# A fused pre-norm decoder layer: experts' units over the whole period, third layer norm and gate in halves, residual in two buffers

## The chip, the cores and the metric

One core of a Trainium2 chip runs the kernel. The metric is the device time of one execution in microseconds, the median of several runs. TensorE multiplies matrices into PSUM, VectorE, ScalarE and GpSimd compute elementwise (the first two read PSUM), and SyncE starts the loads. Each engine works through its own queue in order and waits for the others on semaphores.

## What is computed

The reference takes x of 128 sequences x 64 tokens x 128 features and a context of the same shape. Cut to what matters:

```
x = x + agent_attention(layernorm(x))            # 16 heads of 64, 8 agents per sequence, two softmaxes
x = x + cross_attention(layernorm(x), context)   # 16 heads of 8, causal mask, softmax
x = x + experts(layernorm(x))

def experts(x):
    scores = softmax(x @ gate_w.T)               # 16 experts in 4 groups of 4
    # a group counts the sum of its two best; the two best groups stay;
    # in them the two best experts get their softmax score as weight
    h = silu(x @ We1 + be1) * (x @ We3 + be3)    # 64 wide, each of the 16 experts
    y = sum over experts of weight * (h @ We2 + be2)
    z = (silu(x @ ws1 + bs1) * (x @ ws3 + bs3)) @ ws2 + bs2   # shared expert, 128 wide
    return y + z
```

All experts are computed for all tokens; the weights of those not chosen are zero.

## The kernel before

A group is 16 sequences, 1024 tokens, eight tiles of 128 tokens, and there are eight groups. `run` (L287) calls each engine's `both(e, g)` for nine periods: (None, 0), then (e, e + 1) for e = 0 to 6, then (7, None). In a period the experts of group e run beside the attentions of group g; `nxt` is the group after g, whose first steps (context, first layer norm, agent's moments M) are prepared at the end. The order of each engine's queue is the order of the calls in its `both`, written by hand: TensorE's at L714, ScalarE's at L959, VectorE's at L1256, GpSimd's at L398.

The experts' work is 18 units, nine for each half of the tokens: unit k = 0 and 9 are the shared expert, the others a pair of experts. `unit` (L518) calls `up` (six matmuls of 512 columns, two PSUM banks H1 and H3, high and low parts of the operands apart), `weight` (one matmul that spreads the pair's weights, bank C) and `down_to` of the unit before (eight matmuls; the ninth unit adds the bias; bank Y). `silu` (L882) is ScalarE's part, `hidden` (L1152) VectorE's: `hidden_3` adds the bias and multiplies, `weighted` multiplies by the weights.

Before the units come the third layer norm and the gate, for all eight tiles at once: `norm("e")`, GpSimd's power, `apply("e")`, the turn into xnT3, the scores, `gate_shift` (L1090), ScalarE's exponential, `gate` (L1098: groups, two rounds of the best expert, weights), the turn of the weights (L755). The attention's steps are, in order: values V, `scores_1`, `scores_2` with `soften`, the keys KT with `K_moved`, the turn of the probabilities with `normalise_2`, `pool_tokens`, the agent's values UT, U, `Ya`, the second layer norm `norm("a")` with `apply("a")`, the turn xnT2, the queries QT, four `scores(u)` with `maxima` (row maxima from four banks), the shifts' turn mT, four rounds of `scores_T`, exponentials, `values`, `turn_O`, `project`.

PSUM has eight banks. `RINGS` gives each tile a bank of a ring and `wait_free` makes TensorE wait until the tile before it in that bank was read. Attention has a ring of four; H1, H3, C and Y have one bank each. Outside the units the four are lent: H1 and H3 to the next group's context, xn and M (ring f), C to mT, O, OT (ring o), Y to Yx. So no unit can run while the transposed scores run: units 13 to 16 stand between the four `scores(u)`, and 17 behind them. The residual is xr, the residual after cross-attention xe, and the result is written into xn3's buffer (xo).

## Time and profile before

| what | value |
|---|---|
| median of 3 runs | 1292.38 us (1291.53 to 1292.47) |
| profiled execution | 1290.0 us, span 1288.3 us |
| TensorE matmul busy | 1069.6 us, 83% |
| VectorE busy | 646.9 us, 50% |
| ScalarE busy | 456.3 us, 35% |
| GpSimd busy | 116.5 us, 9% |
| mean granted clock of TensorE | 0.878 of 2.4 GHz |
| loads of ScalarE's tables | 16 of 1.28 us |

The span goes from the first to the last instruction. The busy times are shares over stages with different limits, so the stages are read one by one: windows give each engine's busy time in a stretch, the list of waits says what released an engine, the timeline shows single instructions with the idle time before them. A granted clock of 1.0 is 2.4 GHz, of 0.5 1.2 GHz; a mean between them is a mixture of the two.

### The profile page before, as it was taken

The page shows a single profiled execution, that of the slowest core. Times are in us where ns is not written, and L with a number is a line of the kernel's source. Part 1 is how long each engine was busy: PE and PEld are TensorE (multiplying, and loading weights), DVE is VectorE, ACT ScalarE, POOL GpSimd, SP SyncE. Part 2 cuts the span into 40 slices and gives each one's busy share as a digit, 9 for nine tenths or more (in the row PEclk, how much of TensorE's full clock was granted, in tenths as well). Part 3 has the DMA queues.
Part 4 walks back from the last instruction along what each step waited for, and adds up shares of the span by engine and source line. Part 5 has one row for each costly group of instructions (what it writes and reads, how often), then busy time and mean ns, then how long its engine had stood idle before and what let it go on. Part 6 is the DMA issues. An engine that isn't in the chain of part 4 may idle for free.

```text
span 1288.3 us, 26430 instructions
## 1 busy us (share of the span) xinstructions
PE 1069.6 (83%) x11562; PEld 892.9 (69%) x11629; DVE 646.9 (50%) x1633; ACT 456.3 (35%) x790; POOL 116.5 (9%) x117
## 2 busy tenths in 40 slices
PE   6657879988798969988799887989699887998687
PEld 5644767787676858677676876768586776767565
DVE  2535276624657166542757246571665427561353
ACT  4432453234422353234432344223432345322221
POOL 7100010002000020001000020000200010000100
PEclk9788889978899889988899788998899888995589
DMA  6100010001000010000100010000100000000000
GB/s 164 34 1 2 2 34 1 10 10 34 1 9 10 2 34 1 10 10 2 34 9 2 10 34 1 9 10 2 33 1 10 10 2 1 9 10 2 1 1 17
DMA packets 28404, 18.50 MB, mean 14 GB/s; under 512 B 7393, under 2 KB 26882, under 8 KB 28290
## 3 DMA queue, kind: packets, MB, share of 16 engines
q1 hardware_dynamic: 26402, 12.35, 3.6%
q0 software_dynamic: 1280, 4.20, 1.1%
q8 instruction: 92, 1.51, 0.5%
q10 hardware_dynamic: 608, 0.27, 0.1%
q14 instruction: 22, 0.18, 0.0%
HBM read 12.62 MB, written 4.19 MB: 13 GB/s over the span
## 4 chain that ended last, share of the span: by engine, by line
PE 65%; DVE 20%; ACT 7%; POOL 4%; issue 3%; DVEq 0%; another core or an unknown queue 0%; POOLq 0%; ACTq 0%
PE banks L508 8%; PE banks L651 6%; PE banks L634 5%; PE banks L497 4%; PE banks L498 4%; PE banks L499 4%; PE banks L695 3%; DVE xn L1086 3%; PE banks L539 3%; PE banks L467 3%; ACT PXUT L943 3%; PE banks L626 3%; DVE sil L1172 2%; PE banks L604 2%; PE banks L775 2%
## 5 line engine op out<-in xcount | busy, mean ns | idle before, releaser
L887 ACT ACTIVATE sil<-banks,b 128x512 f32<-128x512 f32 x144 | 99.5, 691 | 247.2 <-PE banks L499 244.5
L508 PE MATMUL banks<-w,hT 128*128 128x128 f32 x1152 | 156.7, 280 | 29.1 <-DVE xn L1185 18.0
L1172 DVE SCALAR_TENSOR_TENSOR sil<-banks,b,sil 128x512 f32<-128x512 f32 x128 | 95.8, 748 | 167.1 <-ACT sil L887 154.9
L508 PEld LDWEIGHTS banks<-w,hT 128*128 128x128 f32 x1152 | 153.5, 196 | 31.6 <-DVE xn L1185 18.5
L1240 DVE RECIPROCAL rx<-banks 128x32 f32<-128x32 f32 x32 | 11.4, 358 | 243.1 <-PE banks L651 243.1
L943 ACT ACTIVATE PXUT<-banks 128x512 f32<-128x512 f32 x128 | 69.4, 609 | 154.8 <-PE banks L634 154.8
L1179 DVE TENSOR_TENSOR hT<-sil,banks 128x512 f32<-128x512 f32 x128 | 88.0, 687 | 15.1 <-remote 11.0
L1223 DVE TENSOR_REDUCE mx<-banks 128x8 f32<-128x512 f32 x128 | 79.5, 684 | 26.5 <-PE banks L604 26.5
L467 PE MATMUL banks<-ident,xn 128*128 128x128 f32 x192 | 38.2, 365 | 56.5 <-DVE xn L1086 56.5
L497 PE MATMUL banks<-xnT3l,w1h 128*128 128x512 f32 x144 | 77.7, 540 | 7.6 <-ACT sil L887 6.4
L695 PE MATMUL banks<-pooled,A 128*128 128x128 f32 x512 | 73.6, 303 | 12.2 <-ACT M L880 10.3
L396 POOL TENSOR_TENSOR norm_a<-norm_a,mhalf 128x8 f32<-128x8 f32 x16 | 26.5, 1656 | 623.2 <-DVE norm_a L1078 623.2
L651 PE MATMUL banks<-Vx,PXUT 128*64 128x18 f32 x2048 | 79.1, 228 | 2.9 <-ACT PXUT L943 2.9
L651 PEld LDWEIGHTS banks<-Vx,PXUT 128*64 128x64 f32 x2048 | 75.9, 162 | 7.6 <-issue 5.1
L634 PEld LDWEIGHTS banks<-KQ 32*128 32x128 f32 x2048 | 74.7, 226 | 8.5 <-issue 8.5
L695 PEld LDWEIGHTS banks<-pooled,A 128*128 128x128 f32 x512 | 69.4, 216 | 15.3 <-ACT M L880 12.9
L634 PE MATMUL banks<-KQ 32*128 32x64 f32 x2048 | 79.5, 314 | 0.0
L467 PEld LDWEIGHTS banks<-ident,xn 128*128 128x128 f32 x192 | 31.5, 191 | 59.2 <-DVE xn L1086 36.3
L497 PE MATMUL banks<-xnT3l,w3h 128*128 128x512 f32 x144 | 61.5, 427 | 5.2 <-DVE sil L1172 4.5
L498 PE MATMUL banks<-xnT3h,w1l 128*128 128x512 f32 x144 | 60.6, 421 | 0.0
L499 PE MATMUL banks<-xnT3h,w1h 128*128 128x512 f32 x144 | 60.0, 417 | 0.0
L498 PE MATMUL banks<-xnT3h,w3l 128*128 128x512 f32 x144 | 58.0, 403 | 0.0
(203 smaller groups left out, 1858.3 us busy)
## 6 DMA issues: line engine op xcount, KB each, us to landing
xin<-in_x SPq DMA_DIRECT2D x8, 512.0 KB, 4.5
cin<-in_ctx SPq DMA_DIRECT2D x8, 512.0 KB, 5.8
out_x<-xn POOLq DMA_DIRECT2D x16, 256.0 KB, 2.8
KQ<-in_L_attn_Wqkv SPq DMA_DIRECT2D x3, 512.0 KB, 5.2
KQ<-in_L_ffn_We SPq DMA_DIRECT2D x2, 512.0 KB, 4.3
KQ<-in_L_attn_Wo SPq DMA_DIRECT2D x1, 512.0 KB, 7.9
w<-in_L_ffn_We SPq DMA_DIRECT2D x1, 512.0 KB
KQ<-in_L_ffn_ws SPq DMA_DIRECT2D x2, 64.0 KB, 4.4
```

The costliest lines, as they stand in the source:

```text
L467: last = turn_over(ps(name)[:, P * t:P * t + P], src[:, 4 * n + t, :], ident[:])
L497: mm(ps(name)[:], wh[:, 2 * p:2 * p + 2, :], xl, start=True, stop=False)
L498: mm(ps(name)[:], wl[:, 2 * p:2 * p + 2, :], xh, start=False, stop=False)
L499: mm(ps(name)[:], wh[:, 2 * p:2 * p + 2, :], xh, start=False, stop=True).then_inc(fulled(name), 1)
L508: mm(ps(name)[:, P * t:P * t + P], hT[:, k % 2, P * t:P * t + P], w2[:, pair[k], :], start=(n == 0 and t == 0), stop=False, skip_group_che ...
L634: last = mm(ps(name)[:, c0:c0 + S], Kx[rr, j, b, :], Qx[rr, S * b:S * b + S], start=False, stop=True, skip_group_check=True, tile_position ...
L651: last = mm(ps(name)[64 * r:64 * r + 64, o0:o0 + w], PT[:, XQ * (u % 2) + j // 2, c0:c0 + S], Vx[:, 4 * u + k, j, :], start=True, stop=True)
L695: last = mm(ps(f"M_{n}")[:, P * k:P * k + P], A[:, 4 * (n % 4) + k, :], pooled[:], start=True, stop=True)
L887: nc.scalar.activation(sil[:, k % 2, :], ps(f"H1_{k}")[:], ACT.Silu, bias=b1[:, pair[k]:pair[k] + 1]).then_inc(sil_ready, 1)
L943: nc.scalar.activation(PT[:, k % (2 * XQ), :], ps(f"ST_{k}")[:], ACT.Exp).then_inc(ex_ready, 1)
L1172: V.scalar_tensor_tensor(sil[:, k % 2, :], ps(f"H3_{k}")[:], b3[:, p:p + 1], sil[:, k % 2, :], ALU.add, ALU.mult).then_inc(hid_ready, 1)
L1179: V.tensor_tensor(hT[:, k % 2, :], sil[:, k % 2, :], ps(f"C_{k}")[:], ALU.mult).then_inc(hT_ready, 1)
```

## The change

1. The four banks of attention serve all of attention, the third layer norm's turn, the gate and the weights' turn; H1, H3, C and Y belong to the units alone. `attention_tiles` writes out the order of the tiles for every period.
2. The units are spread: `unit(e, 0)` opens the period, units 14 to 17 stand in the four rounds of transposed scores.
3. Third layer norm and gate work on halves of four tiles. Half 0 of group g is done at the end of the period in which g's cross-attention ends; half 1 at the start of the next one. `gate` is split into `gate_groups`, `gate_best` (twice) and `gate_weights`.
4. The residual has two buffers by turns, xr[g % 2], in which the sums are made in place; xe and xo are gone.
5. The keys (`keys_of`, `K_moved`) move behind unit 9, the next group's first norm and its turn move ahead of the transposed scores.

```diff
+        if e is None:
+            add(g, "ctxT_0", "ctxT_1", "xnT1_0", "xnT1_1", *[f"M_{k}" for k in range(8)])
+        add(g, *[f"V_{k}" for k in range(4)])
+        add(e, "xnT3_1")
+        add(g, "s1_0", "s1_1", "s2_0")
+        add(e, "combS_0", "gate_1")
...
+        for u in range(UX):
+            add(g, *[f"ST_{XQ * u + q}" for q in range(XQ)])
+            if u:
+                add(g, f"OT_{u - 1}")
+            add(g, f"O_{u}")
+            if u == UX - 1:
+                add(g, "xnT3_0")
+            add(n, f"M_{2 * u}", f"M_{2 * u + 1}")
+            if u:
+                add(g, f"Yx_{u - 1}")
+        add(g, "gate_0", f"OT_{UX - 1}", f"Yx_{UX - 1}")
```

TensorE's order, from the start of a period:

```diff
+                unit(e, 0)
                 if g is not None:
                     pe.wait_ge(ctxT_ready, 2 * g + 2)
                     for n in range(4):
                         values_of(g, n)
                 if e is not None:
+                    turn_3(e, 1)
...
+                    turn_weights(e, 0)
+                unit(e, 1)
+                if e is not None:
+                    gate_scores(e, 1)
                 if g is not None:
                     scores_1(g, 2)
                     scores_1(g, 3)
                     scores_2(g, 1)
+                unit(e, 2)
+                unit(e, 3)
+                if g is not None:
+                    turn_probs(g, 0)
+                unit(e, 4)
...
+                unit(e, 9)
                 if g is not None:
                     keys_of(g, 0)
                     keys_of(g, 1)
+                unit(e, 10)
                 if g is not None:
                     pe.wait_ge(xn_ready, 2 * g + 2)
                     four(g, "xnT2_0", xn, 0)
                     four(g, "xnT2_1", xn, 1)
                 unit(e, 11)
...
+                    queries(g)
+                unit(e, 12)
+                if g is not None:
                     pe.wait_ge(Kx_ready, 2 * g + 2)
+                    scores(g, 0)
+                    scores(g, 1)
+                unit(e, 13)
+                if g is not None:
+                    scores(g, 2)
+                    scores(g, 3)
+                    if nxt is not None:
+                        front_ctx(nxt)
+                        front_xn(nxt)
+                    turn_shifts(g)
+                    pe.wait_ge(V_ready, 4 * g + 4)
                 for u in range(UX):
                     if g is not None:
+                        scores_T(g, u)
+                    unit(e, 14 + u)
+                    if g is not None:
+                        if u:
+                            turn_O(g, u - 1)
+                        values(g, u)
+                    if u == UX - 1:
+                        if e is not None:
+                            down_to(e, UNITS - 1)
+                        if g is not None:
+                            turn_3(g, 0)
                     if nxt is not None:
+                        front_M(nxt, (2 * u, 2 * u + 1))
+                    if g is not None and u:
+                        project(g, u - 1)
+                if g is not None:
+                    gate_scores(g, 0)
+                    turn_O(g, UX - 1)
+                    project(g, UX - 1)
```

VectorE's order:

```diff
                 else:
+                    hidden(e, 0)
+                    gate_best(e, 0, 1)
+                    gate_weights(e, 0)
+                    apply_e(e, 1)
                 if g is not None:
                     soften(g, 0)
+                hidden(e, 1)
                 if e is not None:
+                    gate_shift(e, 1)
                 if g is not None:
                     soften(g, 1)
+                hidden(e, 2)
                 if e is not None:
+                    gate_groups(e, 1)
                 if g is not None:
                     normalise_2(g, 0)
+                hidden(e, 3)
                 if g is not None:
                     normalise_2(g, 1)
                     for q in range(Q):
                         sums_1(g, q)
+                if e is not None:
+                    gate_best(e, 1, 0)
+                hidden(e, 4)
+                if e is not None:
+                    gate_best(e, 1, 1)
+                    gate_weights(e, 1)
+                for k in range(5, 8):
                     hidden(e, k)
...
+                hidden(e, 9)
+                result(e, 0)
+                if g is not None:
+                    apply_a(xr[g % 2], 2 * g + 2, lambda: hidden(e, 10))
...
                 if nxt is not None:
                     dve.wait_ge(x_loaded, 16 * nxt + 16)
+                    norm_a(xin)
+                hidden(e, 12)
+                if g is not None:
+                    maxima(g, 0)
+                    maxima(g, 1)
+                hidden(e, 13)
+                if nxt is not None:
+                    apply_a(xin, 2 * nxt + 1)
+                if g is not None:
+                    maxima(g, 2)
+                    maxima(g, 3)
+                    split_shifts(g)
+                if nxt is not None:
+                    pool_queries(nxt)
                 for u in range(UX):
+                    hidden(e, 14 + u)
+                    if g is not None:
+                        if u == UX - 1:
+                            apply_e(g, 0)
+                        normalise_O(g, u)
...
+                result(e, 1)
+                if g is not None:
+                    gate_shift(g, 0)
+                    add_x(g, UX - 1)
+                    norm_e(g, 1)
+                    gate_groups(g, 0)
+                    gate_best(g, 0, 0)
```

ScalarE's order, where exponentials and silu now alternate:

```diff
+                silu(e, 0)
...
+                    weights_moved(e, 0)
+                silu(e, 1)
                 if g is not None:
                     exp_agent(g, 0)
                 if e is not None:
+                    exp_gate(e, 1)
                 if g is not None:
                     exp_agent(g, 1)
+                silu(e, 2)
...
+                if g is not None:
+                    K_moved(g, 0)
+                    K_moved(g, 1)
                 silu(e, 10)
...
                 for u in range(UX):
+                    if g is not None:
+                        for q in range(XQ):
+                            exp_x(g, XQ * u + q)
+                    silu(e, 14 + u)
```

## Rows read from the trace of the kernel before

**Rows 1.** Windows by period: length, busy time of each engine, granted clock, DMA.

```profile
153.92:301.29 147.37, 126.69 (x1437) 106.16 (x1445) 79.34 (x203) 55.33 (x97) 11.48 (x8) 0.90 0.04 12
...
1050.34:1205.09 154.75, 131.44 (x1356) 108.88 (x1364) 73.71 (x179) 48.99 (x85) 9.67 (x7) 0.80 0.02 5
...
1205.09:1288.30 83.21, 61.27 (x321) 49.81 (x324) 38.57 (x93) 18.21 (x27) 5.71 (x5) 0.81 0.02 7
```

**Rows 2.** Windows, same columns: stages A, B, D and E, then E of period (6,7).

```profile
449.86:482.75 32.89, 21.44 (x186) 18.39 (x187) 22.18 (x74) 16.30 (x29) 6.48 (x4) 0.81 0.12 33
...
482.75:523.97 41.22, 38.03 (x275) 32.31 (x279) 25.28 (x55) 13.79 (x23) 2.44 (x2) 0.96 0.01 1
...
534.60:557.17 22.57, 21.17 (x248) 15.90 (x252) 19.26 (x37) 4.52 (x7) 0.00 (x0) 1.00 0.01 2
...
557.17:599.77 42.60, 37.14 (x641) 33.59 (x641) 9.75 (x34) 17.10 (x33) 2.43 (x2) 0.87 0.03 8
...
1157.87:1205.09 47.22, 40.84 (x568) 35.06 (x568) 5.08 (x15) 10.66 (x21) 0.07 (x1) 0.54 0.02 7
```

**Rows 3.** Waits of TensorE: us in total, times, longest.

```profile
PE banks L467 <- DVE xn L1086: 56.5, 17, 7.3
PE banks L755 <- DVE combs L1150: 43.9, 8, 5.6
```

**Rows 4.** Timeline of TensorE: start, us, instruction, idle time before it and releaser.

```profile
456.24 1.94 PE L467 MATMUL banks<-ident,xn 128*128 128x128 f32 x8 [3.43 <-DVE xn L1086]
...
522.75 1.42 PE L508 MATMUL banks<-w,hT 128*128 128x128 f32 x8 [2.25 <-DVE xn L1185]
...
562.66 1.09 PE L467 MATMUL banks<-ident,xn 128*128 128x128 f32 x8 [2.51 <-DVE xn L1086]
```

**Rows 5.** Windows, same columns as rows 1: behind two of those waits.

```profile
524.00:527.00 3.00, 3.00 (x13) 2.72 (x12) 0.00 (x0) 1.17 (x2) 0.00 (x0) 0.52 0.29 87
...
566.00:575.00 9.00, 9.00 (x101) 8.06 (x100) 1.91 (x3) 2.86 (x6) 0.00 (x0) 0.52 0.01 2
```

**Rows 6.** Timeline of VectorE: gate operations of 128x64 and of 128x128.

```profile
470.24 0.23 DVE L1111 TENSOR_TENSOR ps<-gate 128x64 f32<-128x64 f32 x1
...
474.77 0.29 DVE L1136 TENSOR_TENSOR oh<-oh,down 128x128 f32<-128x128 f32 x1
...
475.09 0.29 DVE L1137 TENSOR_REDUCE g<-oh 128x8 f32<-128x128 f32 x1
```

**Rows 7.** Timeline of VectorE: a unit's product, four maxima, eight normalisings.

```profile
486.78 0.75 DVE L1172 SCALAR_TENSOR_TENSOR sil<-banks,b,sil 128x512 f32<-128x512 f32 x1 [1.12 <-PE banks L499]
...
487.56 0.69 DVE L1179 TENSOR_TENSOR hT<-sil,banks 128x512 f32<-128x512 f32 x1
...
534.68 2.48 DVE L1223 TENSOR_REDUCE mx<-banks 128x8 f32<-128x512 f32 x4 [1.03 <-PE banks L604]
...
560.47 2.14 DVE L1086 TENSOR_SCALAR xn<-xin,norm_a 128x128 f32<-128x128 f32 x8 [1.79 <-POOL norm_a L396]
```

**Rows 8.** Timeline of ScalarE: table load, silu, keys' copies, exponentials.

```profile
469.80 1.28 ACT L887 ACT_TABLE_LOAD   x1
...
471.10 0.69 ACT L887 ACTIVATE sil<-banks,b 128x512 f32<-128x512 f32 x1
...
473.44 4.73 ACT L908 ACTIVATE KQ<-banks,plane 128x512 f32<-128x512 f32 x8
...
560.17 2.07 ACT L943 ACTIVATE PXUT<-banks 128x512 f32<-128x512 f32 x4 [0.69 <-PE banks L634]
```

**Rows 9.** Timeline of TensorE: two tiles of M, starts of two units.

```profile
581.07 1.95 PE L695 MATMUL banks<-pooled,A 128*128 128x128 f32 x16
...
1239.19 0.48 PE L497 MATMUL banks<-xnT3l,w1h 128*128 128x512 f32 x1
...
1241.72 0.48 PE L497 MATMUL banks<-xnT3l,w1h 128*128 128x512 f32 x1
```

More of the change, by code:

```diff
@@ L74, in decoder_block @@
     place = {}
-    for ring, (names, n) in RINGS.items():
-        for at, name in enumerate(names):
-            k = at % n
-            place[name] = (ring, k, at // n, len(range(k, len(names), n)), at)
+    for ring, (tiles, n) in RINGS.items():
+        for at, tile in enumerate(tiles):
+            place[tile] = (ring, at % n, at // n, tiles[at - n] if at >= n else None)
     with ExitStack() as ctx:
@@ L712, in front_M, with turn_3, gate_scores @@
                     moments(g, n)
+            def turn_3(g, c):
+                pe.wait_ge(xn3_ready, 2 * g + c + 1)
+                four(g, f"xnT3_{c}", xn3, c)
+            def gate_scores(g, c):
+                name = f"gate_{c}"
+                wait_free(pe, g, name)
+                pe.wait_ge(xnT3_ready, 2 * g + c + 1)
+                for t in range(QT):
+                    t0 = P * (QT * c + t)
+                    last = mm(ps(g, name)[:, E * t:E * t + E], xnT3[:, t0:t0 + P], gwT[:], start=True, stop=True)
+                last.then_inc(fulled(g, name), 1)
@@ L797, in both @@
-                for k in range(7, 11):
-                    unit(e, k)
+                unit(e, 10)
                 if g is not None:
```

725 lines of the change are left out of this document (344 added, 381 removed).

## The prediction

> **What bounds the kernel now.** I read the windows by period first. Six middle periods run from 153.92 to 1050.34, 149.4 us each; the seventh with both halves of the work takes 154.75, the last 83.2 [rows 1]. TensorE is busy for 126.7 of 147.4 us in one of them, VectorE for 79.3, ScalarE for 55.3: TensorE is the bound, and what a change can win is its idle time and the time at the lower clock. Next I cut the middle period from 449.86 to 599.77 into five stages [rows 2]: A, to the first turn of the agent's probabilities; B, to the second turn of xn; C, to the end of the first scores; D, to the start of the transposed scores; E, to the last projection. A has 11.5 us without TensorE and E 5.5; B and D together 4.6. The list of waits names the two large ones: the turn of xn or xn3 for VectorE's normalising, 56.5 us in 17 places, and the turn of the experts' weights for the gate, 43.9 us in 8 [rows 3]. In time order that is 3.43 us for xn3 at 456.24 and 2.51 for the next group's xn at 562.66 [rows 4]. Behind such waits the granted clock falls to its lower level, 1.2 GHz: 0.52 in the 3 us after the wait of 2.25, and 0.52 for 9 us after the wait of 2.51 [rows 4, 5]. At half clock 9 us hold some 4.5 us of work.
>
> **What the change aims at, and what it moves.** Gate and third layer norm are cut by tokens. The first half is done at the end of the period before, so unit 0 opens a period, and four units (14 to 17) go from stage D into E. I sum stage by stage, since every new wait sits in one.
>
> **Stage A.** The path is VectorE's queue. Before, from the last projection to xn3 it is 6.4 us (456.24 - 449.86), of which 2.14 are the eight normalisings [rows 4, 7]. In the new order VectorE does, after the last projection: the residual and half the statistics, about 1.9; gate_groups of half 0; gate_best; unit 0's product; the other gate_best; the weights; only then the normalising of half 1, on which turn_3 stands in TensorE's queue. Linked gate operations of 128x128 follow each other at 0.32 us (0.29 busy), one of 128x64 is busy 0.23 [rows 6]; so a halved one costs about 0.26, not 0.16. By that, gate_groups (ten linked, eight others at about 0.1) is 3.2, gate_best 1.55 and 1.3, the weights 1.25. The sum is 1.9 + 3.2 + 1.55 + 0.75 + 1.3 + 1.25 + 1.1 = 11.0 us. TensorE has unit 0's first matmuls (1.4 of a unit's 2.52) and the values (2.95, from 449.86 to 452.8) to cover it: a wait of about 6.6 us. Bounds on a halved operation are 0.16 and 0.32, so 8.5 to 13 for the chain. Behind turn_3 stand the agent's scores and all units. ScalarE then adds one more: silu(2) follows exp_agent and exp_gate, so a table load (1.30 us from its start to the next activation) comes before it [rows 8], and unit 3 waits about 1.4. So A = 32.9 - 11.5 idle + 5.2 (units 2 and 3, at 2.52 each, and unit 1's remainder [rows 9]) - 3.4 (estimate: keys and halves of three tiles that left) + 6.6 + 1.4 = 31.2, against 32.9.
>
> **Stage B.** Two units less and the keys added: 41.2 - 5.0 + 1.9 = 38.1. Of the old costs the low clock at its head (about 2.5) and the wait of 2.25 for the result [rows 4] go: 33.3. New waits: gate_groups(1), 3.2, stands in VectorE's queue ahead of normalise_2(0), on which the turn of probabilities waits: 3.3. gate_best(1) stands ahead of hidden(4): 1.7 at unit 5, and 0.3 at the weights' turn. The keys' copies, 4.73 us for eight on ScalarE [rows 8], now stand after KT and ahead of silu(10); before, they lay under the gate's wait. hidden(10) is called half way in apply_a, so the second half of xn waits for it: agent_out, unit 9 with its bias (4.4), KT_0 (0.75), copies (4.75), silu (0.75), product (1.4: 0.75 and 0.69 [rows 7]), half the normalising (1.15) are 13.2 us, of which TensorE fills 8.3 (unit 9, keys, unit 10). Wait 4.9. B = 33.3 + 10.2 = 43.5; by adding the pieces one by one in order I get 43.2 and keep that.
>
> **Stage C.** Work as before, low clock after a wait as before: 10.5.
>
> **Stage D.** With four units gone the maxima are bare. Each lot of four takes 2.48 us, and scores(u+1) needs the banks of scores(u). The chain on VectorE is maxima(0) 2.5, the remainder of scores(1) after its last free bank 1.4 (estimate), maxima(1) 2.5, hidden(13) 1.4, the next group's normalising 2.15, put ahead of maxima(2) [rows 7], maxima(2) 2.5, rest of scores(3) 1.45, maxima(3) 2.5, the shifts' split 1.05 (four at 0.26), turn 0.6 (eight transposes of f32 are 1.09 [rows 4]) and copy 1.05 (a copy of half the size is 0.59 [rows 8]): 19.1 us, against 22.6 with some 4.6 units in it. The work of TensorE that stays is 21.2 - 4.6 x 2.52 = 9.6 [rows 2, 9], so 9.5 us of waiting, the longest about 4.4 before scores(3).
>
> **Stage E.** Before 42.6 with 37.1 busy at a mean clock of 0.87 [rows 2]: 26% of it at the lower level, half lost, 5.5; 31.6 of work at the upper. Minus the xn turn (1.0), plus four units, the last product with its bias, turn_3 and gate (13.1), plus 1.3 of waits at the end = 45.0. A round has room: four exponentials 2.07, two table loads 2.6, silu 0.69, three copies 1.5 are 6.9 on ScalarE, in a round of about 10.3 [rows 8]; two of M's tiles are 1.95 on TensorE [rows 9]. So the ten loads more per period lie under TensorE except where A counts one. One bank ring for all costs nothing here, as each release falls before its reuse.
>
> **The clock.** The waits in D are as long as those that were followed by the lower level before. For D and E together the bounds are 0 and about 6.2 (1.5 for 3 us at 0.52, 4.7 for 9 us at 0.52 [rows 5]). I take 4.7, as the nearest row is the wait at the same place, ahead of the transposed scores.
>
> A middle period is 31.2 + 43.2 + 10.5 + 19.1 + 45.0 + 4.7 = 153.7, 4.3 longer; six are +26. Period (6,7): no normalising in D (-2.15), no M in E (-7.8, estimated from four times 1.95), 2.4 more at the ring's releases: 146.1 against 154.75 [rows 1], -8.6. Last period: unit 4 would start some 22.8 us in (11.0 for the chain of A, 11.8 for turn_3, the weights' turn and units 1 to 3), against 34.1 before (1239.19 - 1205.09 [rows 9]); the second half's gate gives back 4.2; the result's wait of 2.25 goes: -9. First, without units: a round waits for its exponentials in the open, and gate half 0 is done there: 0 to +6, I take +3. Sum +11.4 on the span of 1288.3: 1299.7. Around the span lie 1.7 us (1290.0), and the median stands 2.4 above that execution: 1304.
>
> **Page against row.** The Trainium skill, "ScalarE: Activation LUTs", section "What ACT_TABLE_LOAD costs", gives about 2.66 us for a switch, with a drain of 1.38 behind the load of 1.28. The trace has 1.28 for the load and the next activation 0.02 later [rows 8], so it doesn't agree. By the page the sum would be that of rival 3.
>
> **Rivals.**
> 1. Faster: the units in E and the matmuls in D keep the clock at the upper level. For it: the 9 us at the lower level ended inside E, whose mean is 0.87 [rows 2], with no unit there. Against it: both waits whose clock is shown, 2.25 and 2.51, were followed by a fall [rows 4, 5]. Price: 6.2 less in seven periods (4.7, and 1.5 in C): -43, 1261. It decides the sign from 1.7 us a period, since 12 us over seven periods is all that I forecast; 1258 to 1288.
> 2. Slower still: the level stays low through E. For it: in period (6,7) E runs at 0.54 for 47 us [rows 2]. Against it: it had neither units nor M. Half of E low would add some 10 us in seven periods: 1374; a round more, 4.5: 1336.
> 3. Slower by the switches: behind each load ScalarE stays empty once more as long as the load takes (1.28). Then silu(17) and silu(2) come 1.3 later ahead of waits of TensorE, twice in seven periods: 1304 + 18 = 1322. Against it: the 0.02 us of [rows 8]. This is the page's rule above.
> 4. The change is cheaper than its parts: half an operation costs half. Then both gate chains are 2.5 shorter: 1304 - 35 = 1269.
>
> **How the numbers follow.** Forecast 0.47 (its own range 1290 to 1322), rival 1 0.30, rival 2 0.12, rival 3 0.03, rival 4 0.08. A measurement tells 0.2%, 2.6 us, from no change. Faster: 0.38 less the edge of rivals, 0.36; same: the forecast's lower end, 0.09; slower: 0.55. Range 1262 to 1336: it takes in half the clock's bound on both sides and rival 4, and leaves out rival 1's lowest 0.04 and rival 2's larger half.
>
> **What would show it.** Right: TensorE waits 6 to 8 us for turn_3 behind VectorE's xn3, 4 to 5 us for xnT2 with the keys' copies ahead of silu(10), and in D two waits for maxima of 2.5 and 4.4; unit 0 opens each period without a wait; some 90 table loads. Wrong: a period under 149 us, D under 18, or a clock over 0.93 in E. The step I hold weakest is the clock.

## The result, and the profile after

The changed kernel takes 1309.49 us (median of four executions, 1308.48 to 1311.47); the kernel before took 1291.95 beside it on the same chip. The ratio is 1.0145, with a 95% interval of 1.0121 to 1.0168: slower by 1.5%. The forecast was 1304 and slower. The profiled execution took 1309.68 us; its span is 1307.9 against 1288.3.

The windows by period come first, with the columns of [rows 1]: the first period, the six middle ones in one row, period (6,7), the last.

```profile
0.00:164.02 164.02, 119.57 (x1289) 98.04 (x1290) 61.32 (x158) 59.28 (x100) 35.19 (x59) 0.84 0.16 40
164.02:1084.30 920.28, 766.95 (x8608) 627.66 (x8666) 511.65 (x1482) 411.03 (x653) 69.95 (x54) 0.91 0.04 11
1084.30:1236.25 151.95, 124.07 (x1358) 99.98 (x1366) 79.57 (x223) 61.85 (x98) 10.41 (x9) 0.85 0.02 5
1236.25:1307.90 71.65, 52.60 (x310) 42.26 (x313) 41.32 (x122) 20.75 (x30) 4.15 (x5) 0.91 0.04 12
```

A middle period is 920.28 / 6 = 153.4 us; before it was 149.4 [rows 1]. The sum of the differences is +10.1 (first) + 24 (six middles) - 2.8 (period (6,7)) - 11.6 (last) = +19.7, which is the difference of the spans (19.6). TensorE's work hardly changed, its idle time grew: in a middle period it is busy for 127.8 us and idle for 25.6, in the one of [rows 1] for 126.7 and 20.7. Next the five stages of the middle period from 470.01 to 624.18, A to E in order, cut as in [rows 2].

```profile
470.01:500.39 30.38, 21.45 (x196) 18.35 (x197) 20.30 (x76) 14.85 (x25) 5.20 (x4) 0.83 0.16 44
500.39:544.14 43.75, 35.59 (x255) 29.78 (x257) 30.17 (x84) 17.51 (x30) 2.40 (x2) 0.92 0.03 7
544.14:554.99 10.85, 10.85 (x90) 7.93 (x90) 5.26 (x19) 3.72 (x6) 1.66 (x1) 0.85 0.00 0
554.99:577.03 22.04, 15.48 (x183) 8.56 (x184) 15.48 (x31) 4.02 (x7) 0.00 (x0) 0.85 0.00 1
577.03:624.18 47.15, 45.51 (x716) 40.80 (x721) 14.02 (x39) 28.58 (x43) 2.47 (x3) 0.96 0.01 2
```

Units were meant to fill TensorE's idle time. In E they do: 1.6 us idle against 5.5. But A still has 8.9 us without TensorE, B has 8.2 where it had 3.2, and D has 6.6 where it had 1.4 [rows 2]. The list of TensorE's waits (us in total, times, longest) names them:

```profile
PE banks L489 <- DVE xn L1182: 60.7, 8, 9.4
PE banks L489 <- DVE xn L1174: 43.3, 9, 5.5
PE banks L620 <- DVE mx L1325: 29.2, 61, 2.1
PE banks L591 <- DVE PXUT L1310: 24.6, 8, 3.3
PE banks L521 <- ACT sil L946: 10.5, 8, 1.5
PE banks L532 <- DVE hT L1280: 6.1, 8, 0.8
```

Of the 43.9 us for the weights' turn [rows 3] 1.2 are left. In their place stand the third norm's second half (L1182, the scalings of `apply_e`; 7.3 us a period, 9.4 in the last), the second norm's turn (L1174, 4.6 a period), the maxima (L1325) and the agents' probabilities (L1310, 3.3 in six periods of the seven). The first of these is explained by VectorE's timeline in the next middle period (start, us, instruction); it shows where each part of its chain begins: the groups of half 0, the first choice, unit 0's product, the second choice, the weights' first step, and last the scalings on which TensorE waits.

```profile
626.22 0.21 DVE L1202 TENSOR_REDUCE g<-gate 128x4 f32<-128x64 f32 x1
...
629.33 0.22 DVE L1233 TENSOR_REDUCE g<-gate 128x4 f32<-128x64 f32 x1
629.59 0.23 DVE L1234 TENSOR_TENSOR oh<-gate,g 128x64 f32<-128x64 f32 x1
...
630.88 0.75 DVE L1262 SCALAR_TENSOR_TENSOR hT<-banks,b,sil 128x512 f32<-128x512 f32 x1
631.54 0.21 DVE L1233 TENSOR_REDUCE g<-gate 128x4 f32<-128x64 f32 x1
...
632.82 0.22 DVE L1246 TENSOR_TENSOR gate<-oh 128x64 f32<-128x64 f32 x1
...
634.01 1.11 DVE L1182 TENSOR_SCALAR xn<-xr,norm_e 128x128 f32<-128x128 f32 x4
```

TensorE's timeline shows its wait for this chain and, in the period above, the two waits of stage B:

```profile
504.30 1.09 PE L591 MATMUL banks<-ident,PXUT 128*128 128x128 f32 x4 [3.31 <-DVE PXUT L1310]
...
544.14 1.97 PE L489 MATMUL banks<-ident,xn 128*128 128x128 f32 x8 [4.64 <-DVE xn L1174]
...
635.17 1.11 PE L489 MATMUL banks<-ident,xn 128*128 128x128 f32 x4 [7.32 <-DVE xn L1182]
```

Behind all three TensorE is at its lower level: four turns take 1.09 us at 504.30 and 1.11 at 635.17, where four take 0.63 at the upper one, and eight take 1.97 at 544.14 instead of 1.09. So a wait can cost more than its own length. It need not: in three of the seven periods the four turns of the probabilities run at the upper level, in two of them behind the same wait of 3.33, and in just these three unit 5 then waits 1.36 us for VectorE, which the slower matmuls cover in the others. The wait of 4.64 has its cause on ScalarE: the keys' eight copies stand ahead of unit 10's silu, and VectorE does unit 10's product before it scales the second half of xn.

```profile
536.17 4.73 ACT L967 ACTIVATE KQ<-banks,plane 128x512 f32<-128x512 f32 x8 [0.29 <-PE banks L711]
540.75 0.74 ACT L946 ACTIVATE sil<-banks,b 128x512 f32<-128x512 f32 x1
```

### The profile page after: what moved, and what is told of

The parts are those of the page before. It is cut to its first block, busy times and chain, and to the rows that moved or that the text cites. A ratio compares the mean times of both kernels' runs of the same rounds, so it can differ in the third digit from the quotient of the medians.

```text
span 1307.9 us, 26930 instructions
## 1 busy us (share of the span) xinstructions
PE 1063.2 (81%) x11554; PEld 867.9 (66%) x11629; DVE 693.9 (53%) x1985; ACT 552.9 (42%) x878; POOL 119.7 (9%) x125
## 4 chain that ended last, share of the span: by engine, by line
PE 61%; DVE 24%; ACT 9%; issue 3%; POOL 2%; POOLq 0%; DVEq 0%; another core or an unknown queue 0%
PE banks L532 8%; PE banks L719 5%; PE banks L658 5%; DVE mx L1325 5%; PE banks L521 4%; PE banks L675 4%; PE banks L522 4%; PE banks L523 4%; PE banks L489 3%; PE banks L563 3%; PE banks L628 3%; ACT KQ L967 3%; PE banks L650 2%; DVE sil L1273 2%; PE banks L770 2%
## 5 line engine op out<-in xcount | busy, mean ns | idle before, releaser
L532 PEld LDWEIGHTS banks<-w,hT 128*128 128x128 f32 x1152 | 158.4, 200 | 10.8 <-DVE hT L1280 7.0
L489 PE MATMUL banks<-ident,xn 128*128 128x128 f32 x192 | 42.6, 382 | 104.2 <-DVE xn L1182 60.7
L1325 DVE TENSOR_REDUCE mx<-banks 128x8 f32<-128x512 f32 x128 | 79.5, 683 | 53.6 <-PE banks L628 53.6
L521 PE MATMUL banks<-xnT3l,w1h 128*128 128x512 f32 x144 | 80.5, 559 | 10.5 <-ACT sil L946 10.5
L939 ACT COPY M<-banks 128x512 f32<-128x512 f32 x80 | 47.2, 590 | 88.9 <-PE banks L719 63.5
L939 ACT COPY KQ<-banks 128x256 f32<-128x256 f32 (+1 forms) x64 | 30.6, 477 | 120.1 <-PE banks L489 92.6
L675 PE MATMUL banks<-Vx,PXUT 128*64 128x18 f32 x2048 | 68.5, 215 | 5.6 <-ACT PXUT L1002 5.6
L675 PEld LDWEIGHTS banks<-Vx,PXUT 128*64 128x64 f32 x2048 | 65.4, 143 | 10.7 <-ACT PXUT L1002 6.3
L620 PE MATMUL banks<-maskb,pick 32*64 32x512 bf16 x512 | 46.1, 444 | 29.7 <-DVE mx L1325 29.2
L658 PEld LDWEIGHTS banks<-KQ 32*128 32x128 f32 x2048 | 61.7, 191 | 6.9 <-issue 6.9
L658 PE MATMUL banks<-KQ 32*128 32x64 f32 x2048 | 66.1, 278 | 0.0
L939 ACT COPY PXUT<-banks 128x512 f32<-128x512 f32 x64 | 35.9, 588 | 62.8 <-PE banks L603 41.9
```

What stands on the lines that cost most here:

```text
L489: last = turn_over(ps(g, name)[:, P * t:P * t + P], src[:, 4 * n + t, :], ident[:])
L521: mm(ps(e, name)[:], wh[:, 2 * p:2 * p + 2, :], xl, start=True, stop=False)
L532: mm(ps(e, name)[:, P * t:P * t + P], hT[:, k % 2, P * t:P * t + P], w2[:, pair[k], :], start=(n == 0 and t == 0), stop=False, skip_group_ ...
L658: last = mm(ps(g, name)[:, c0:c0 + S], Kx[rr, j, b, :], Qx[rr, S * b:S * b + S], start=False, stop=True, skip_group_check=True, tile_posit ...
L675: last = mm(ps(g, name)[64 * r:64 * r + 64, o0:o0 + w], PT[:, XQ * (u % 2) + j // 2, c0:c0 + S], Vx[:, 4 * u + k, j, :], start=True, stop= ...
L939: cp(dst, ps(g, name)[:] if src is None else src).then_inc(ready, 1)
```

## The experiments

All are edits of the changed kernel. Its median is 1309.49, and every gain below is taken from there; the medians of the kernel before beside the three sets of experiments are 1291.07 to 1291.37, so the sets can be compared. A period is a middle one unless said otherwise. The theory: the change is slower because it trades the wait for the gate's weights for four others that lie in the open, each given by a place in a queue. The rivals: they share one resource and only move; the clock decides; the table loads cost.

**The keys' copies out of the way.**

```diff
                         values_of(g, n)
+                    keys_of(g, 0)
+                    keys_of(g, 1)
...
                 unit(e, 9)
-                if g is not None:
-                    keys_of(g, 0)
-                    keys_of(g, 1)
                 unit(e, 10)
...
                         V_moved(g, n)
+                    K_moved(g, 0)
+                    K_moved(g, 1)
...
-                if g is not None:
-                    K_moved(g, 0)
-                    K_moved(g, 1)
                 silu(e, 10)
```

> Edit against the changed kernel: the keys' two matmuls are issued right behind the values' matmuls of the second attention, where TensorE waits 7.3 us a period for the second half of the third norm's turns, and the keys' two copies stand on ScalarE right behind the values' copies, instead of ahead of the silu of unit 10. Theory (the waits of the changed kernel lie in the open one after another, and each is a queue position): the wait of 4.63 us at the second turn of the second norm falls under 1, the keys' 1.4 us of matmuls fill the wait at the third norm's turns; 5 to 6 us a period, 35 to 45 us less than the changed kernel, about 1270. Rival (the second norm's turn is paced by VectorE's and ScalarE's work for units anyway, so what the copies release only moves the wait): under 1.5 us a period, under 10 us in all, about 1300 to 1309, and the wait at the second turn stays over 3.

Measured: 1269.96 (ratio to before 0.9839, 0.9805 to 0.9873), 39.5 us less; a usual period is 146.9. TensorE's timeline of this kernel:

```profile
474.51 1.11 PE L489 MATMUL banks<-ident,xn 128*128 128x128 f32 x4 [5.29 <-DVE xn L1180]
...
532.02 1.09 PE L489 MATMUL banks<-ident,xn 128*128 128x128 f32 x8 [1.90 <-DVE xn L1172]
```

The wait at the second norm's turn fell from 4.64 to 1.90, not below 1, and the eight turns behind it run at the upper level (1.09 us). B went from 43 to 38.4 us: 2.7 are the wait, and 1.9 the keys' matmuls themselves. The wait at the third norm's turn fell by 2.0 (7.3 to 5.3), but the keys' matmuls stand there now, so A stayed at 30.5. The gain is inside the theory's range, and the theory holds in the main: one move took 2.7 us off a wait, and the turns behind it kept the upper level. Not all of the usual period's gain is its doing: E takes 45.55 us in four periods instead of 47.2, behind the same wait of 0.8 us for the last unit, and 51.7 in one; on the mean of the six E is as before, and a period gains 5.3 us, 4.5 in B and 0.8 in C, which begins with those eight turns.

**The second half's gate later.** On VectorE the normalising of the probabilities goes ahead of the groups; groups and choices stand behind hidden 4, 5 and 6, `sums_1` behind them; the turn of the weights is behind unit 7.

```diff
                 hidden(e, 2)
-                if e is not None:
-                    gate_groups(e, 1)
                 if g is not None:
                     normalise_2(g, 0)
                 hidden(e, 3)
...
+                hidden(e, 4)
+                if e is not None:
+                    gate_groups(e, 1)
+                hidden(e, 5)
                 if e is not None:
                     gate_best(e, 1, 0)
-                hidden(e, 4)
+                hidden(e, 6)
```

> Edit against the changed kernel: the second half's gate on VectorE is taken apart and put behind later units (the normalising of the agents' probabilities ahead of its groups; groups behind hidden 4, the choices behind hidden 5 and 6, the turn of its weights on TensorE behind unit 7). Theory (the wait of 3.33 us at the turn of the probabilities and the 1.4 us of units 5 and 6 are the second half's gate standing ahead of them in VectorE's order): 4 to 5 us a period less, 28 to 35 us, about 1277. Rival (VectorE's work up to the second norm's turn is what counts, and where the gate lies in it changes nothing but the place of the wait): under 1.5 us a period, 1300 to 1309, with the wait at the second norm's turn longer by what the others lost.

Measured: 1270.47 (0.9844, 0.9814 to 0.9874), 39.0 us less. In its timeline of TensorE the wait for the probabilities is nearly gone and the one at the second norm's turn is as long as it was:

```profile
342.89 0.63 PE L592 MATMUL banks<-ident,PXUT 128*128 128x128 f32 x4 [0.19 <-DVE PXUT L1312]
...
380.11 1.97 PE L490 MATMUL banks<-ident,xn 128*128 128x128 f32 x8 [4.63 <-DVE xn L1176]
```

B is 38.0 us. The waits that went add up to 3.1 + 1.4 = 4.5, the stage gave 4.9 (from 43.0 on the mean of six periods), and the four turns now run at the upper level (0.63 us against 1.09). That the second norm's wait would take up the gain is refuted. Stage C, behind that wait, is 0.9 us longer on the mean (11.75). The gain is 4 us above what I expected; period (6,7) alone gave 6.1.

**The third norm's second half ahead of the choice.**

```diff
                     gate_groups(g, 0)
+                    apply_e(g, 1)
                     gate_best(g, 0, 0)
...
                     gate_weights(e, 0)
-                    apply_e(e, 1)
```

> Edit against the changed kernel: the third norm's second half (its four scalings on VectorE) is queued ahead of the first half's choice of experts instead of behind its weights. Theory (the 7.3 us of TensorE's wait at the second half's turns is the part of VectorE's chain that stands ahead of the scalings, and nothing else is late there): the wait falls by the choice and the weights of half 0, about 4.6 us a period, to about 2.7; some 30 us less than the changed kernel, about 1280. Rival (the logits and weights of half 0, now 4.5 us later, are late at the weights' turns instead): gain under 1 us a period, 1302 to 1309, and a new wait of 3 us or more at the weights' turns.

Measured: 1308.17 (1.0113, 1.0057 to 1.0169), 1.3 us less; the executions range from 1296.09 to 1310.83, and the profiled one is the shortest. Its timeline of TensorE shows both things foretold:

```profile
627.44 0.75 PE L489 MATMUL banks<-ident,xn 128*128 128x128 f32 x4 [2.68 <-DVE xn L1182]
...
635.00 0.58 PE L759 MATMUL banks<-identb,combs 128*128 128x128 bf16 x4 [2.47 <-DVE combs L1251]
```

The first wait fell by the 4.6 us that I had worked out, and 2.5 of it came back at the weights' turn: A is 27.4 to 28.9 us instead of 30.5. By the time the rival was nearer; the mechanism is a mixture. Why the other three executions are 10 to 15 us longer than the profiled one no trace shows, and it stays open.

**The scaling between the maxima.**

```diff
                     maxima(g, 0)
-                    maxima(g, 1)
-                hidden(e, 13)
                 if nxt is not None:
                     apply_a(xin, 2 * nxt + 1)
                 if g is not None:
+                    maxima(g, 1)
+                hidden(e, 13)
```

> Edit against the changed kernel: the first norm's scaling of the next batch (four operations, 2.1 us) moves from behind hidden 13 to between the first and the second group of maxima, where VectorE waits for the next scores. Theory (VectorE's four maxima of 5.3 us with the scaling between them are what the scores' stage waits for): 2 us a period, 13 us less, about 1297. Rival (the stage is set by TensorE's scores and their buffers, so that the scaling lies beside the wait anyway): within 3 us of the changed kernel.

Measured: 1315.65 (1.0193, 1.0157 to 1.0229), 6.2 us more: a miss. From the first scores on, VectorE has the shifts ready 1.75 us earlier, close to the 2 that I counted, but stages C and D together are shorter by 0.75 only (32.14 against 32.9). The next batch's turns show where the rest went. First the changed kernel, then this one:

```profile
572.37 1.16 PE L489 MATMUL banks<-ident,cin 128*128 128x128 f32 x8 [0.88 <-DVE mx L1325]
573.57 1.16 PE L489 MATMUL banks<-ident,xn 128*128 128x128 f32 x8
```

```profile
572.10 1.94 PE L489 MATMUL banks<-ident,cin 128*128 128x128 f32 x8 [0.86 <-DVE mx L1325]
573.83 1.91 PE L489 MATMUL banks<-ident,xn 128*128 128x128 f32 x8
```

Behind the same wait the sixteen turns run at half clock, 1.3 us longer from start to end, and the shifts' turn, queued behind them, is late by about 1. In one of the six periods the low level then lasted into E, which took 51.7 us. What VectorE gave, TensorE's clock took back, here and in the sum; of the 6 us of the median the trace shows 4.

**Fewer table loads.** Units 14 to 17 use the exponential in place of silu, so this kernel leaves out a part of the computation: the hidden values of these units are not silu's.

```diff
-                nc.scalar.activation(sil[:, k % 2, :], ps(e, f"H1_{k}")[:], ACT.Silu,
+                nc.scalar.activation(sil[:, k % 2, :], ps(e, f"H1_{k}")[:], ACT.Silu if k < 14 else ACT.Exp,
```

> Edit against the changed kernel: units 14 to 17 use the exponential in place of silu, so that ScalarE changes its table eight times less in a period (the rest of the computation is as it was; the hidden values of these four units are not silu's). Theory (a change of table costs its load of 1.28 us on ScalarE with next to nothing behind it, and the exponentials' stage is paced by TensorE at its low clock, with 0.8 us of wait for the last units): 0 to 6 us less in all, 1303 to 1309. Rival (each change also drains ScalarE, as in the prediction's third rival, with more than 1.2 us beside the load): 18 us or more less in all, 1291 or below, and the exponentials' stage shorter by 2.5 us or more a period.

Measured: 1291.65 (1.0004, 0.998 to 1.0029), 17.8 us less, at the edge of what the rival gave, and E is 44.7 us against 47.2. By the total the rival seemed to win. But the four rounds of exponentials are as long as before (10.2 us from one to the next). The difference is at the last unit's output; TensorE's timeline, first of the changed kernel, then of this one:

```profile
615.80 2.08 PE L532 MATMUL banks<-w,hT 128*128 128x128 f32 x8 [0.79 <-DVE hT L1280]
617.67 1.78 PE L538 MATMUL banks<-b2x,combT 128*128 128x128 f32 x8
```

```profile
609.56 1.16 PE L532 MATMUL banks<-w,hT 128*128 128x128 f32 x8
610.55 1.06 PE L538 MATMUL banks<-b2x,combT 128*128 128x128 f32 x8
```

A wait of 0.79 us is gone, and the sixteen matmuls behind it run at the upper level, 1.6 us shorter until the next one starts: together 2.4 of the 2.5. Two causes fit, the loads or the wait with its clock. The next kernel parts them.

**One tile of M under that wait, all loads kept.**

```diff
                     if u == UX - 1:
+                        if nxt is not None:
+                            front_M(nxt, (6,))
                         if e is not None:
                             down_to(e, UNITS - 1)
...
-                        front_M(nxt, (2 * u, 2 * u + 1))
+                        front_M(nxt, (7,) if u == UX - 1 else (2 * u, 2 * u + 1))
```

> Edit against the changed kernel: in the last round of exponentials one of M's two tiles (0.98 us of TensorE) is issued ahead of the last unit's output instead of behind the third norm's turn; ScalarE copies it ahead of the third norm's copy. The silu and all table loads stay. Theory (the kernel with four units on the exponential was shorter not by its table loads but because the last unit's output no longer waited 0.8 us, and the clock no longer fell behind that wait): the wait of 0.8 us goes, the 1.6 us of half clock behind it goes too, the exponentials' stage falls from 47.2 to 44.7 or less; 10 to 18 us less in all, about 1293. Rival (each of the eight loads costs about 0.3 us by itself, and the wait is beside the point): 0.8 us a period at most, 0 to 6 us, about 1304 to 1309.

Measured: 1296.61 (1.0046, 1.0026 to 1.0067), 12.9 us less. Its timeline of TensorE at the same place:

```profile
613.88 1.16 PE L722 MATMUL banks<-pooled,A 128*128 128x128 f32 x8
614.87 1.06 PE L535 MATMUL banks<-w,hT 128*128 128x128 f32 x8
615.77 1.06 PE L541 MATMUL banks<-b2x,combT 128*128 128x128 f32 x8
```

E is 44.68 us in four of the six periods, to 0.01 that of the kernel with 55 loads less (88 against 33), and 49.3 in the other two, whose first round ran at half clock. So in the middle periods the loads are free once that wait is filled, and a wait of 0.8 us had cost 2.5. Of the 5 us that the exponential gave beyond this, 3.5 are E of period (6,7), where this edit does nothing, since no M is left to move. There the loads are not free: 2.3 of the 3.5 lie at the last output, where the same wait and half clock stand, and 1.2 in the second and third round, which take 9.1 us with the loads and 8.5 without.

**M ahead of the values in the first period.**

```diff
                             turn_O(g, u - 1)
+                        if nxt is not None and (e is None):
+                            front_M(nxt, (2 * u, 2 * u + 1))
                         values(g, u)
```

> Edit against the changed kernel: in the first period, which has no units, the front matmuls M of the next batch stand ahead of each pair of values instead of behind, so that TensorE has work under ScalarE's exponentials; the other periods are as they were. Theory (the first period is 10 us longer than in the kernel before because the rounds of exponentials without units leave TensorE idle in the open, 1.1 to 2.2 us at a time, and the low clock follows): 7 to 10 us less, about 1300, and the granted clock of the stage from the first transposed scores up to the last projection goes up. Rival (ScalarE sets these rounds: exponentials, copies of M and of the values; the order on TensorE is free): within 2 us of the changed kernel.

Measured: 1298.56 (1.0077, 1.0049 to 1.0104), 10.9 us less; two of nine executions are at 1308. The first unit starts at 153.51 instead of 164.02. TensorE's timeline, a round of the changed kernel and one of this:

```profile
142.75 2.05 PE L675 MATMUL banks<-Vx,PXUT 128*64 128x18 f32 x64 [1.12 <-ACT PXUT L1002]
144.73 3.66 PE L719 MATMUL banks<-pooled,A 128*128 128x128 f32 x16
```

```profile
133.79 2.02 PE L723 MATMUL banks<-pooled,A 128*128 128x128 f32 x16
135.74 2.05 PE L679 MATMUL banks<-Vx,PXUT 128*64 128x18 f32 x64
```

M's tiles at half clock (3.66 us) are at full clock (2.02) once no wait of 1.12 us stands ahead of them. The granted clock from the first transposed scores to the first unit is 0.93 instead of 0.77. That fits the theory, but the order alone does not keep the clock up: in the profiled execution of the five edits below, which has the same order and the same wait of 0.76 us ahead of M's first pair, three of the four pairs of M's tiles took 3.6 us again, and the first unit started at 165.37.

**Units back between the scores.** One kernel moves units 14 and 15 there and leaves two rounds bare; the other moves 14 only, has unit 15 in the first round and leaves the second bare. Both also put M ahead of the values in the bare rounds (the second kernel in the whole first period too) and the next group's scaling behind the first maxima, as in the edit above that put it between them. The edit shown is that of the first.

```diff
                     scores(g, 0)
-                    scores(g, 1)
                 unit(e, 13)
                 if g is not None:
+                    scores(g, 1)
+                unit(e, 14)
+                if g is not None:
                     scores(g, 2)
+                unit(e, 15)
+                if g is not None:
                     scores(g, 3)
...
-                    unit(e, 14 + u)
+                    if u >= 2:
+                        unit(e, 14 + u)
```

> Edit against the changed kernel: units 14 and 15 go from the first two rounds of exponentials back between the scores (one unit behind each of the first three scores), M ahead of the values in those two rounds; rounds 2 and 3 keep units 16 and 17. Theory (the scores' stage is paced by VectorE's bare maxima, 22.0 us with 8 of TensorE's idle in it, and a unit's matmuls fit there): the scores' stage grows by less than 3 us, the exponentials' stage shrinks by two units, 8 us a period net if the clock follows, about 1255. Rival (the exponentials' stage is paced by ScalarE, not by TensorE, once the units are gone, or stays at the low clock): the two stages together change by less than 2 us, about 1297 to 1320.

> Edit against the changed kernel: unit 14 goes from the first round of exponentials back behind the second scores, unit 15 moves from the second round to the first, and the second round has no unit and M ahead of the values; the next batch's first scaling stands behind the first group of maxima. Theory (the scores' stage has room for a unit beside its bare maxima, a round without a unit is 8.8 us against 10.2, and with a unit in the first round the clock does not stay low as it did when both early rounds were bare): the scores' stage 21 to 22 us instead of 23.5, the exponentials' stage 45.8 instead of 47.2; 3 us a period, about 1287. Rival (what falls in the scores' stage comes back as low clock in the first round, 13.4 us instead of 10.2): 0 to 1 us a period, 1300 to 1309.

Measured for the first: 1284.65 (0.9956, 0.9925 to 0.9987), 24.8 us less; for the second 1285.12 (0.9975, 0.9944 to 1.0007), 24.4 less. In the first, the stretch from the first scores to the transposed scores is with two units more not longer but 2.4 us shorter, 21.16 against 23.54, and its granted clock is 1.00. Yet the exponentials' stage with two units less is 46.87 long, hardly shorter than with four. Its windows, from the first scores to the transposed scores and from there to the first unit, and the head of the second on TensorE's timeline, say why:

```profile
540.43:561.59 21.16, 17.92 (x262) 11.79 (x262) 18.72 (x36) 5.40 (x9) 0.45 (x1) 1.00 0.01 2
561.59:608.46 46.87, 43.78 (x690) 38.84 (x691) 11.21 (x35) 22.08 (x37) 2.47 (x3) 0.89 0.01 2
```

```profile
563.20 3.69 PE L662 MATMUL banks<-KQ 32*128 32x64 f32 x64
567.65 3.75 PE L723 MATMUL banks<-pooled,A 128*128 128x128 f32 x16 [0.76 <-ACT PXUT L1013]
```

The first bare round runs at half clock (3.69 and 3.75 us for what takes 2.01 and 2.02 in the next), the second at full. So the stretch of the scores became shorter (0.8 of the 2.4 is what the scaling gave alone), what the exponentials' stage lost in work went to the clock, and the total lies between the two expectations; 5.5 us of the 24.8 are the first period, where M's new order in two rounds acts. No run tested the units' place without the scaling's. With unit 15 in the first round, E is 44.2 in five of six periods and 48.7 in one; the stretch of the scores gave only 0.8, what the scaling gives alone. The scores thus gave less than I had counted (1.5 to 2.5) and the exponentials more (1.4): the same total comes by another way, and that 1285 lies close to the 1287 expected is in part luck.

**Five edits at once**: keys, gate later, third norm first, scaling between the maxima, M first.

> Five edits against the changed kernel at once: keys early, the third norm's second half ahead of the first choice, the second half's gate later, the first norm's scaling between the maxima, M ahead of the values in the first period. Theory (the waits stand one after another in the open and are queue positions, so their prices add): 15 to 18 us a period less, 110 to 130 us in all, 1180 to 1200. Rival (they share one resource, VectorE up to the second norm's turn, or the clock takes back what they give): less than half of it, over 1250.

Measured: 1184.98 (0.917, 0.9128 to 0.9212), 124.5 us less than the changed kernel and 8.3% less than the one before. The single gains add up to 39.5 + 39.0 + 1.3 - 6.2 + 10.9 = 84.5: by the medians they are worth 40 more together. By the profiled executions it is 21 (94.6 singly, 115.5 together), as the profiled one was the shortest of the third norm's kernel and the longest of this one; only these 21 can be looked for in traces. In stage A they are some 2 us a period: A takes 25.9 on the mean, 4.6 less, where the keys alone had given 0.1, the third norm alone 2.0 and the later gate 0.4. The keys' matmuls lie in the time that the norm's edit had left as a wait for the weights: TensorE's total for that turn is 5.8 us in two places, against 23.9 in nine with the norm's edit alone. B has nothing of them: 33.6 us is what the keys and the later gate give added up. C and D have 1.4 a period: 30.7 us together against 32.9, where the scaling between the maxima and the keys had given 0.75 each and the later gate had cost 0.8.

**The version that beats both**: keys, third norm, gate later, unit 14 between the scores with a bare second round and the scaling behind the first maxima, M first in the first period and under the last unit's output.

> The edits that shortened the kernel, together: keys early, the third norm's second half ahead of the first choice, the second half's gate later, one unit back between the scores and a bare second round, M ahead of the values in the first period, and one of M's tiles ahead of the last unit's output. Theory (queue positions add up): 136.7 us a period of the five edits less 2.5 for the last unit's wait and 1.5 to 3 for the unit between the scores, 131 to 133 us a period, 1150 to 1165. Rival (with fewer waits elsewhere the remaining ones are taken over by the low clock or by VectorE): within 10 us of the five edits' 1185.

Measured: 1167.93 (0.9059, 0.9025 to 0.9092), 9.4% less than before and 10.8% less than the changed kernel. It stayed 3 us above what I expected. A usual period is 133.0 us, the upper end of what was counted. The windows of the six middle periods (133.2 each, clock 0.97) and of period (6,7):

```profile
166.50:965.92 799.42, 726.75 (x8606) 594.34 (x8666) 507.81 (x1482) 395.98 (x641) 70.24 (x54) 0.97 0.05 13
965.92:1101.99 136.07, 119.18 (x1358) 96.83 (x1366) 79.20 (x223) 59.46 (x96) 10.55 (x9) 0.90 0.02 5
```

The units over the whole period thus beat the order of before by 9%, once the other queues are in step. How much of it is due to the units and how much to the moves is not shown: none of these moves was tried on the kernel before, which has waits of the same kind [rows 3].

## Why the prediction was right, and where it was not

- **Sign and size.** 1304 was forecast, 1309.49 measured, inside the forecast's own range. A middle period was forecast at 153.7 and is 153.4. The sum was short by 8 us on the span, and the median does not stand 2.4 above the profiled execution as it did before. The misses are -2 us in the six middle periods, +7.1 in the first, +5.8 in period (6,7) and -2.6 in the last; that they and the 2.4 partly cancel is luck.
- **Stage A: 31.2 forecast, 30.4 measured.** The chain of VectorE is 10.9 us from 624.2 to 635.1, forecast 11.0, part by part: groups 3.1 (3.2), first choice 1.55 (1.55), second 1.3 (1.3), weights 1.2 (1.25). An operation of half the size is busy 0.22 and the next one starts 0.26 later, against 0.29 and 0.32 for the whole one [rows 6]. The fourth rival falls with these rows: half an operation costs four fifths. The wait is 7.3 instead of 6.6, and silu 2 makes unit 3 wait 1.46 (1.4).
- **Stage B: 43.2 and 43.75.** The waits: 3.31 (3.3), 1.36 (1.7; in three periods of the seven, not in the one shown), 4.64 (4.9). The edits with the keys and with the later gate showed that these are causes: the one shortened its wait from 4.64 to 1.90, the other took out the first two, and B fell by 4.5 and 4.9 without a new wait in it. I counted no low clock behind the first of them, and in four periods there is some: four turns of 1.09 us instead of 0.63. The one behind the third, eight turns of 1.97 instead of 1.09, lies in C and was counted there.
- **Stages C, D and E: 10.5, 19.1 and 45.0, with 4.7 of clock for the last two; measured 10.85, 22.04 and 47.15.** D and E together are 69.2 against 68.8, but the step from the wait ahead of the transposed scores to the low clock did not come about as forecast: the clock's term has about the right size in other places, and that is luck. In D the second and the fourth scores, behind waits for maxima, run at half clock, the third at the upper level:

```profile
563.82 1.04 PE L628 MATMUL banks<-KQ 32*64 32x256 f32 x32
569.16 2.33 PE L628 MATMUL banks<-KQ 32*64 32x256 f32 x32
```

  So the maxima behind them start 1.4 us later than in my chain, twice, and that is 2.8 of the 2.9 us that D is longer. In E the kernel with M's tile ahead of the last output takes 44.68, so what stood above my 45.0 is the wait of 0.79 us at that output, which I had not counted, with half clock behind it. I had named a clock above 0.93 in E as a sign against me, and it was 0.96. The longest wait for maxima is 2.06 and not 4.4: from the end of the second scores to the next freed bank it is 6.6 us, as my chain has it, but unit 13 and the third scores fill 4.5 of them.
- **First period: +3 with a bound of 6, measured +10.1.** The step that failed is this term. It counted the exponentials in the open and took the clock as given; the edit with M ahead of the values gave 10.9 back, and its rows show that half clock is the greater part, some 1.6 us for each of the four pairs of M's tiles.
- **Period (6,7): -8.6 forecast, -2.8 measured.** I took out M's whole 7.8 us from E. Read from the trace: the rounds without M are 9.1 us against 10.2, so a round gives 1.1 and not 1.95, since TensorE then waits 0.45 us for VectorE in the shifts' product and the rest goes elsewhere in the round; and the first round is 2.8 us longer, at half clock behind a wait of 3.77 for the shifts. 4 times 1.1 less 2.8 is 1.6; E is 1.1 shorter than in a middle period. In the kernel with fewer table loads such a round takes 8.5 us and the wait of 0.45 is gone, so 0.6 of what M's round did not give went to the loads. No run tested the rest alone.
- **Last period: -9 forecast, -11.6 measured.** Unit 4 starts after 22.4 us, forecast 22.8. Of the 2 us that I let the second half's gate give back on balance, 0.2 came.
- **The rivals.** The clock did not stay up (first rival), and E was not low throughout (second). The third said that ScalarE stays empty behind a table load as long as the load takes. Where its next work is ready, the changed kernel's ScalarE goes on at once, as in these rows:

```profile
582.11 1.28 ACT L946 ACT_TABLE_LOAD   x1
583.40 0.69 ACT L946 ACTIVATE sil<-banks,b 128x512 f32<-128x512 f32 x1
```

  The Trainium skill, "ScalarE: Activation LUTs", section "What ACT_TABLE_LOAD costs", gives 1283 ns for the load and 1380 ns of drain besides. The first figure agrees to the digit. The section does not say on which side of the load the drain lies, and the second figure has no counterpart in these traces on either: the exponential ahead of the load ends 0.02 us before it, the silu starts 0.01 us behind it, and in the middle periods the kernel with 88 loads and a filled wait has the same E as the one with 33. The measurement decides.

## What to carry to other kernels

Work cut finer and spread fills idle time only where the queues of the other engines let it: before moving work onto a bound engine, list what stands ahead of each thing that it waits for, and move that first. Price a wait by its length and by what the clock does behind it. And judge such edits together: those that shortened stage A by 0.1, 2.0 and 0.4 us alone shortened it by 4.6 together.

## What the runs showed of the hardware

A wait as short as 0.8 us was followed by the lower clock: the sixteen matmuls behind it took 3.5 us until the next one started instead of 1.9, so the wait cost three times its length. It need not be so. In one of the six middle periods of the changed kernel and in four of the kernel with the keys early the same wait, 0.80 us at the same place, was followed by the upper level; from the latter:

```profile
603.63 1.16 PE L532 MATMUL banks<-w,hT 128*128 128x128 f32 x8 [0.80 <-DVE hT L1278]
604.62 1.06 PE L538 MATMUL banks<-b2x,combT 128*128 128x128 f32 x8
```

What makes the difference stays open. The same stage of one kernel takes one of a few lengths, as E in that kernel with 45.5, 47.2 or 51.7 us, and the executions of one kernel can be 10 us apart.
